# First attention block: two passes interleaved unit by unit, row sums turned on TensorE, the maxima's mask added inside VectorE's reduction

## The reference, cut to what matters

```python
qh = (layernorm(x) @ Wq.T + bq)   # per head: 256 x 16
kh = (ctx @ Wk.T + bk); vh = (ctx @ Wv.T + bv)
scores = qh @ kh.T / sqrt(16)                  # per batch and head: 256 x 256
scores = where(mask[:, None] == 0, -1e10, scores)
x = x + (softmax(scores) @ vh).concat_heads() @ Wo.T + bo
```

## Time and profile before

| what | value |
|---|---|
| median of three runs | 2055.79 us |
| the profiled execution | 2057.15 us |
| its span on the core | 2055.3 us |
| busy: PE, PEld, DVE, ACT, POOL | 1573.8, 1345.9, 876.4, 550.3, 336.8 us |
| the block in question | from 29.3 us (L483) to 369.75 us (end of the last L557) of the span |
| one batch in its middle | 37.43 us |

### The profile page before, as it was taken

One profiled execution on the slowest core, in us unless ns is written; L12 is line 12 of the kernel. 1 busy time (PEld: TensorE's weight loads), 2 busy tenths in 40 slices (PEclk: granted clock), 3 DMA queues, 4 the chain that ended last, 5 costly groups with the idle time before them and its releaser, 6 DMA issues. The chain is left out here.

```text
span 2055.3 us, 32700 instructions
## 1 busy us (share of the span) xinstructions
PE 1573.8 (77%) x11346; PEld 1345.9 (65%) x11346; DVE 876.4 (43%) x1913; ACT 550.3 (27%) x1311; POOL 336.8 (16%) x401
## 2 busy tenths in 40 slices
PE   2799997539991799999994099999999256691775
PEld 2565664429991688888874099999999244581664
DVE  5443542402224566665665011111111235448896
ACT  1233232102221455454441011111111011231553
POOL 1121120030002333332321400000000511004122
PEclk8999999569996799999995599999999678795787
DMA  4344241158132100000003454224470210101000
GB/s 127 59 76 66 48 69 12 59 200 276 39 113 86 61 7 7 7 7 2 2 1 113 148 195 148 103 67 146 148 270 18 76 47 16 34 26 41 6 15 21
DMA packets 118240, 152.13 MB, mean 74 GB/s; under 512 B 15360, under 2 KB 101376, under 8 KB 118016
## 3 DMA queue, kind: packets, MB, share of 16 engines
q1 hardware_dynamic: 101536, 123.86, 19.6%
q0 software_dynamic: 7680, 18.89, 4.1%
q10 hardware_dynamic: 8928, 8.13, 1.1%
HBM read 113.16 MB, written 24.64 MB: 67 GB/s over the span
## 5 line engine op out<-in xcount | busy, mean ns | idle before, releaser
L1271 PEld LDWEIGHTS f_ph<-f_xgT,f_w 128*128 128x128 f32 x3232 | 373.0, 193 | 21.7 <-issue 18.8
L1271 PE MATMUL f_ph<-f_xgT,f_w 128*128 128x128 f32 x3232 | 374.4, 277 | 16.1 <-DMA f_w<-in_f_w 14.9
L1281 PE MATMUL f_py<-f_w,f_hT 128*128 128x256 f32 x992 | 224.6, 379 | 0.0
L1281 PEld LDWEIGHTS f_py<-f_w,f_hT 128*128 128x128 f32 x992 | 183.7, 190 | 22.6 <-issue 0.2
L1342 DVE TENSOR_TENSOR f_hT<-f_ph,f_gate_o 128x512 f32<-128x512 f32 x78 | 54.0, 692 | 309.3 <-ACT f_gate_o L1305 309.3
L1376 POOL DMA_INDIRECT c_yt<-sorted_y,dest x48 | 45.6, 950 | 649.7 <-issue 648.8
L799 ACT ACTIVATE a_work<-a_ps,a_bias 128x128 f32<-128x128 f32 (+1 forms) x256 | 104.1, 419 | 149.0 <-DVE a_bias L879 91.3
L937 POOL TENSOR_TENSOR a_work<-a_work,a_recip 128x256 f32<-128x256 f32 (+1 forms) x128 | 103.1, 827 | 234.3 <-DVE a_recip L894 234.3
L145 PE MATMUL n_tp<-ident,n_xn 128*128 128x128 f32 x160 | 33.1, 384 | 134.9 <-DVE n_xn L125 134.3
L1305 ACT ACTIVATE f_gate_o<-f_ph 128x512 f32<-128x512 f32 x78 | 46.6, 597 | 295.2 <-PE f_ph L1271 295.1
L145 PEld LDWEIGHTS n_tp<-ident,n_xn 128*128 128x128 f32 x160 | 25.8, 196 | 142.7 <-DVE n_xn L125 135.9
(11 more groups left out here) (307 smaller groups left out, 3103.7 us busy)
## 6 DMA issues: line engine op xcount, KB each, us to landing
f_w<-in_f_w SPq DMA_DIRECT2D x72, 1024.0 KB, 7.2
f_xg<-sorted_x SPq DMA_DIRECT2D x62, 128.0 KB, 2.1
sorted_y<-f_yg ACTq DMA_DIRECT2D x62, 128.0 KB, 1.7
a_qs<-a_part SPq DMA_DIRECT2D x96, 64.0 KB, 5.1
a_ks<-a_part POOLq DMA_DIRECT2D x96, 64.0 KB, 5.3
sorted_x<-zeros SPq DMA_DIRECT2D x1, 4992.0 KB, 16.5
a_ctxT<-in_ctxT SPq DMA_DIRECT2D x16, 256.0 KB, 2.7
sorted_x<-zeros SPq DMA_DIRECT2D x1, 2944.0 KB, 10.2
```

What stands on the lines that cost most here:

```text
L1271: mm = pe.matmul(ph[:, q, n, f * P:(f + 1) * P], w[:, s, k, (q * FQ + f) * P:(q * FQ + f + 1) * P], xgT[:, s, k, :], start=(k == 0), stop= ...
L1281: mm = pe.matmul(py[:, s, 0:D], hT[:, s, f, :], w2[:, s, f, :], start=(f == 0), stop=(f == FT - 1))
```

## The change

Both passes now run in one stream. One step of TensorE (`scores(k)`) holds the second pass of unit k (banks 0 and 1, "ST") and the first pass of unit k+9 (banks 2 and 3, "SC"), which is more than a batch ahead. Between the steps stand, by the unit's number within the batch: queries and the turning of sums (0), keys (1), products with V (2, 4, 6, 7, four heads at a time), the spreading of reciprocals (3), the product with Wo (4, 5), the turning of maxima (6), and values (7). Projections run two batches ahead. All loops are unrolled. ST and SC are single: a step waits both for the exponential and for the maximum of the step before.

- q and k are split in two fp32r parts; three products, 48 rows. One head of a unit lies on partitions 0 to 47 and the other on 64 to 111, so the two heads' products use different halves of the array. 6 DMAs for q and 6 for k per batch, twice as large.
- The first pass has no mask product. VectorE adds the mask and takes the maximum in one `tensor_tensor_reduce` of 256 columns, four of them per unit, in place of one `tensor_reduce` of 1024.
- The second pass keeps its mask product (`shut`), 4 per unit.
- Sums: eight fp32 products of `oraw` with a selector of 4 columns, a reciprocal out of PSUM, a widening copy on GpSimd (128 x 1024), eight transposes on TensorE. The eight DMAs per batch are gone.
- Four DMAs (was three) put the maxima back. The start needs three loads before the first product (was seven and the context).

```diff
-            def maxima(b, before):
-                for u in range(U):
-                    dve.wait_ge(s_ready, b * U + (u + 1))
-                    dve.tensor_reduce(top_s[:, :, 2 * u:2 * u + 2].rearrange("p t j -> p j t"),
-                                      ps[:, 2 * (u % 2):2 * (u % 2) + 2, :].rearrange("p j (t k) -> p j t k", t=TB),
-                                      AX.X, ALU.max).then_inc(max_done, 1)
+            def maximum(m):
+                dve.wait_ge(s_ready, m + 1)
+                ...
+                for j in range(2):
+                    for t in range(TB):
+                        a = dve.tensor_tensor_reduce(out=shut_s[:, j, t, :], in0=ps[:, bank(m) + j, t * S:(t + 1) * S],
+                                                     in1=neg[:, m // U % 3, t, :], scale=1.0, scalar=2 * NEG,
+                                                     op0=ALU.add, op1=ALU.max,
+                                                     accum_out=top_s[:, t, j, m % U:m % U + 1])
+                a.then_inc(max_done, 1)
```

```diff
+            def pairs(first, left, right, rows, b, u, opens):
+                for t in range(TB):
+                    for j in range(2):
+                        r = slice(j * HALF, j * HALF + rows)
+                        mm = pe.matmul(ps[:, first + j, t * S:(t + 1) * S], left[r, b % 3, u, t * P:(t + 1) * P],
+                                       right[r, b % 3, u, :], start=opens and t == 0, stop=True, skip_group_check=True)
+                return mm
+
+            def scores(k):
+                m = k + AHEAD
+                if is_unit(m):
+                    if m >= AHEAD:
+                        pe.wait_ge(max_done, m)
+                    elif m >= 2:
+                        pe.wait_ge(max_done, m - 1)
+                if is_unit(k):
+                    ...
+                    if k >= 1:
+                        pe.wait_ge(exp_done, k)
+                    shut(ST, negT, k // U)
+                if is_unit(m):
+                    ...
+                    pairs(bank(m), qs, ks, ROWS, m // U, m % U, True).then_inc(s_ready, 1)
+                if is_unit(k):
+                    ...
+                    pairs(ST, ks, qs, ROWS + 2, k // U, k % U, False).then_inc(st_ready, 1)
```

```diff
+            def turn_sums(b):
+                ...
+                for n in range(NG):
+                    for t in range(TB):
+                        c = (n * TB + t) * G
+                        mm = pe.matmul(ps[:, OB, c:c + G], oraw[:, n, t * P:(t + 1) * P], sel[:, :],
+                                       start=True, stop=True)
+                mm.then_inc(sums_ready, 1)
+
+            for k in steps:
+                i, u = k // U, k % U
+                scores(k)
+                if u == 0 and is_batch(i + 2):
+                    queries(i + 2)
+                if u == 0 and is_batch(i - 1):
+                    turn_sums(i - 1)
+                if u == 1 and is_batch(i + 2):
+                    keys(i + 2)
+                if u == 3 and is_batch(i - 1):
+                    spread_sums(i - 1)
+                if u in (2, 4, 6) and is_batch(i):
+                    weigh(i, u // 2 - 1)
+                if u in (4, 5) and is_batch(i - 1):
+                    output(i - 1, u - 4)
+                if u == 6 and is_batch(i + 1):
+                    turn_maxima(i + 1)
+                if u == 7 and is_batch(i + 2):
+                    values(i + 2)
+                if u == 7 and is_batch(i):
+                    weigh(i, NG - 1)
```

More of the change, by code:

```diff
@@ L199, in attention0 @@
[L199 to L203, removed]
+        neg, negT = sb("neg", [P, 3, TB, S], BF16), sb("negT", [P, 3, TB, S], BF16)
+        part = sb("part", [P, 2, 2, DK, S], F32R)
+        qs, ks = sb("qs", [P, 3, U, S], F32R), sb("ks", [P, 3, U, S], F32R)
+        V = sb("V", [P, 3, TB, H, W])
@@ L231, in every_batch @@
[L231 to L237, removed]
+                    for j in range(DK):
+                        engine.dma_start((qs, ks)[w][j * HALF + t * D0:j * HALF + (t + 1) * D0, b % 3, :, :].bitcast(F32),
+                                         part[:, n, w, j, :].bitcast(F32)).then_inc((q_stacked, k_stacked)[w], 16)
@@ L239, in _ @@
+        steps = range(-2 * U, B * U + 6)
         @block.sync
         def _(sp):
[L241 to L252, removed]
@@ new lines, in queries, with keys @@
+            def queries(b):
+                if b == 0:
+                    pe.wait_ge(qk_in, 16 * 3)
+                if b >= 4:
+                    pe.wait_ge(resid_done, b - 3)
+                project(wq, 0, [xt[:, k, b * S:(b + 1) * S] for k in range(DK)], q_proj)
+            def keys(b):
+                pe.wait_ge(ctx_in[b % 2], 16 * (b // 2 + 1))
+                if b >= 1:
+                    pe.wait_ge(v_out, b)
+                project(wk, 1, [ctxT[:, b % 2, k, :] for k in range(DK)], k_proj)
@@ L427, in batch, with stack @@
-            def batch(b, s, half, last):
-                if not last:
-                    pool.wait_ge(pv_done, b * U + 2)
-                    stack(b + 1, 1 - s)
-            every_batch(pool, batch)
+            def stack(b):
+                if b >= 3:
+                    pool.wait_ge(st_ready, (b - 2) * U)
+                pool.wait_ge(k_high, b + 1)
+                to_stack(pool, 1, 0, b)
+                pool.wait_ge(k_low, b + 1)
+                to_stack(pool, 1, 1, b)
+            pool.memset(ks[:, :, :, :].bitcast(F32), 1.0).then_inc(set_done, 1)
@@ L473, in _ @@
-            split(0, first=True)
-            split_maxima(0)
-            every_batch(act, batch)
+                if b >= 1:
+                    act.wait_ge(mrow_landed, b * 64)
+                act.mul(mpart[:, 0, :], ps[0:H, OB, 0:S], -1.0).then_inc(mhi_done, 1)
+            for k in steps:
+                i, u = k // U, k % U
+                if is_unit(k):
+                    exps(k)
+                if u == 0 and is_batch(i + 2):
+                    high(i + 2, 0, q_proj, q_high)
+                if u == 1 and is_batch(i + 2):
+                    high(i + 2, 1, k_proj, k_high)
+                if u == 6 and is_batch(i + 1):
+                    split_maxima(i + 1)
```

501 lines of the change are left out of this document (249 added, 252 removed).

## The result

| | before | changed |
|---|---|---|
| median of the runs | 2053.42 us (4 runs, 2049.03 to 2058.91) | 2003.88 us (4 runs, 2002.03 to 2009.84) |
| ratio to before | | 0.9762, 95% interval 0.9728 to 0.9796 |
| profiled execution: time, span | 2057.15, 2055.3 | 2009.84, 2008.0 |
| last addition of the block ends | 369.75 | 322.05 |
| span behind it | 1685.6 | 1686.0 |

The forecast was 1999 us, from 1970 to 2038. The kernel before has a fourth run here (2049.03), so its median is 2053.42. All of the gain lies in the block: its end comes 47.7 us earlier, the span is 47.3 shorter. First the stretches of the changed kernel (columns as in the earlier trace rows): one middle batch, two at the end, then the two before the second pass and the second pass whole.

What follows compares the result with a forecast made beforehand. TensorE's own work was taken to bound the block. Start 74, batches 228 and end 11 sum to 313 us against 369.75, 57 less, giving 1999 us; range for eight in ten 1970 to 2038.

Steps and rivals of the forecast that it cites:

- maximum of a unit: VectorE, first pass: four operations of 256 columns with overlapping accumulator reads, 4 x (0.34 + 0.09) = 1.72 us.
- TensorE's own work in a batch: Steps, projections, Wo, sums, transposes and V in one batch: 26 us, against 35 before.
- The middle: The interleaved batches: 30.4 us each against 37.43, eight making 243, or 228 with the edges.
- Units 1 and 2: Together 7.1 us: unit 2's maximum comes only after ScalarE's high part, VectorE's low part and the reciprocal.
- The widening copy: On GpSimd behind the K stack's DMAs: 1.2 us, ending as unit 3's transposes come up, nothing to spare.
- The upper bound of 2.0: Products with V for four heads: 2.0 us if only two column groups run at once; 1.0 was taken.
- The start: Before the second pass: first product at 34, scores at 50, first second-pass unit at 74 us, about 76 before.
- The end: Behind the last unit: 11 us at the full clock, 6 more if TensorE falls to 1.2 GHz.
- VectorE hidden altogether: Rival: low parts and maxima fit into TensorE's gaps, 26 us a batch, 1959 us in all; chance 0.12.
- Small operations without overlap: Rival: VectorE's small operations don't overlap, 0.74 us more per unit, 2025 us in all; chance 0.13.
- the slow reduction: Rival: add-and-maximum takes two cycles per column without overlap, 3.5 us a unit, 2073 us in all; chance 0.07.
- The loss of the clock: Rival: TensorE's mean clock falls to 0.8, 6.5 us more a batch, 2051 us in all; chance 0.06.

Runs made afterwards that it cites:

- the runs with another order: Changed kernel with VectorE's reciprocals, keys' low part and mask preparation reordered in units 0 to 2: 2012.92 us; with GpSimd's widening copy also ahead of the K stack's DMAs: 2001.26 us.
- the best order: Changed kernel with VectorE's small operations reordered in units 0 to 2 and GpSimd's widening copy ahead of the K stack's DMAs: 2001.26 us.
- two of the variants: Changed kernel with V's products ordered for two column groups side by side: 2003.94 us; changed kernel with VectorE's order in units 0 to 2 altered: 2012.92 us.

## Why the prediction was right, step by step

| step | predicted | measured |
|---|---|---|
| first projection | 34 | 32.90 |
| first scores | 50 | 55.79 |
| first second-pass product | 74 | 84.61 |
| maximum of a unit | 1.72 | 1.46 |
| sixteen products with V | 1.0 | 1.07 |
| TensorE's own work in a batch | 26 | 26.25 |
| units 0; 1+2; 3; 4; 5; 6; 7 | 4.8; 7.1; 3.0; 4.1; 3.1; 3.4; 4.1 | 5.01; 6.62; 3.34; 4.03; 3.04; 2.82; 4.12 |
| a batch | 30.4 | 28.98 |
| second pass, eight batches | 228 | 221.5 |
| end | 11, 17 at half clock | 15.9 |
| last addition | 313 | 322.05 |

**The middle** was right as a mechanism, and 1.4 us too long. Of this, 0.8 are the 0.1 a step that I had added for semaphores: the steps as measured hold whatever these cost and add up to 28.98, mine without them to 29.6. The other 0.6 are 1.1 too much in units 1, 2 and 6, less 0.5 too little in units 0 and 3. Most of the 1.1 is the maximum. I had let the accumulator read cost 0.09 us before the next operation; it costs nothing, since it starts with that operation. That is 0.26 per unit, felt where VectorE is last, in units 2 and 6. By the Trainium skill (VectorE: DVE Perf Modes, "The DRAIN you can't avoid") the next operation waits until the pipe is empty, though the same section adds that one that isn't held starts earlier. The trace has 0.345 from start to start at a duration of 0.42, so here the second statement holds and not the first, on which the prediction's rival went.

**Units 1 and 2** wait where I said, behind ScalarE's high part, the low part and the reciprocal. But I thought only of the late maximum. TensorE stood 1.10 us for the reciprocal as well, at the products with V, as the runs with another order show; that time was inside the wait for the maximum, so the step still came out at 6.62.

**The widening copy** had, I wrote, nothing to spare behind the K stack's DMAs. It was late by 1.14 us in each batch (unit 3: 3.34 instead of 3.0).

**V.** The upper bound of 2.0 is excluded: sixteen instructions in 1.07. (Two figures of the prediction don't follow from their terms: twelve paired products in 0.90 make 0.60 for eight, not 0.66, which the trace happened to give; and 2.48 less 1.72 is 0.76, not 0.74. The first is worth 0.5 us of TensorE's work in a batch, the second moves a rival by under 1 us.) The Trainium skill's rule of tiles in different column groups that overlap (TensorE: Matmul & The Clock Gate, "Part 3: Packing small matmuls") is in accord with this.

**The start is the step that failed**, by 10.6 us. Two things were in it. I let the stack land 6.8 us after its last issue, as in the earlier trace rows; the K stack took 11.8 (issued until 43.95, landed at 55.79), where the same stack issued by SyncE took 6.8 to 7.2. The first scores came 5.8 us late by it; GpSimd's queue accounts for 2.7 of these in the mean of the traces, 4.2 at most. And I let the second pass begin when the maxima are back. But in the interleaved program TensorE's order puts the first product of the *second* batch's first pass ahead of it, and behind that the values' projection at half clock: it waited 4.29 us for that batch's K stack at 80.31, then 3.78 for the projection. By the prediction's own 3.7 us the maxima, whose DMAs were issued from 76.91, would have been back at 80.6 (an estimate), so this order cost about 4.0 us. The order of instructions had this; I had only followed the data.

**The end** came out near the half-clock figure, which I had priced and not taken: 0.57 of the clock granted from 306 us on.

The errors partly cancel: +10.6 in the start, -6.5 in the middle, +4.9 in the end is +9.0 at the block's end. The median was 6.0 us below the profiled execution where I had allowed 1.4, so 4.4 remain; with 0.5 from rounding and the rest of the program that is the 4.9 between 1999 and 2003.88. That the total came so near is partly luck: two errors of opposite sign, and a median that happened to lie further below its profiled execution. **The rivals:** VectorE hidden altogether (1959) would need 26 us a batch; the best order reached 27.25. Small operations without overlap and the slow reduction fell with the 0.345. The loss of the clock did not come in the middle of this kernel (it did from 255 us on: 0.89 from 256 to 286), but it was nearer than a chance of 0.06 says: two of the variants lost 1.4 to 1.7 us a batch to it.

## What to carry to other kernels

When two streams are interleaved on one engine, follow that engine's order at the seams: a product that waits for the next batch's transfer holds up everything of this batch behind it. Small operations that share a queue with DMA issues (here a copy of 1.05 us behind six issues of 3.3) are the next bound once the large work is out of the way, and two waits that hide each other must be removed together. Read a releaser as one of several, and compare milestones of the block rather than whole times when the rest of the program varies by more than the effect.

## What the hardware showed that I had not expected

- VectorE's accumulator read (0.08 us) runs beside the next add-and-maximum; 256 columns out of PSUM cost 0.345 us each in a row.
- The same instructions in another order can bring a stretch of half clock into every middle batch, even with TensorE busy all through it (5.00 of 5.00 us at 0.67), and cost 1.4 to 1.7 us each time.
- GpSimd wrote 6144 columns in 5.2 us and copied 1024 broadcast ones in 1.05, cheaper than the estimates of 7 and 1.2.
- Copies of 128 KB within SBUF landed after 9.0 us (median) when GpSimd issued them and after 7.1 when SyncE did, behind the Q stack's; the Q stack's own, of the same size and issued by SyncE in both kernels, landed after 4.6 and 4.5.
